# AdaLN block with an SSM layer and an eight-expert FFN: second modulated state kept as two fp32r parts, its shift folded into biases, b_out added by GpSimd, small VectorE operations moved to a PSUM bank

## The reference, cut to what matters

```python
# x (8, 1024, 128); c (8, 128); eight experts of 128x128
mod = (silu(c) @ wmod).reshape(8, 6, 1, 128)
sa, ca, ga, sb, cb, gb = (mod[:, i] for i in range(6))
ga, gb = guarded(ga), guarded(gb)            # sign * max(abs, 0.25)
h = layernorm(x) * (1 + ca) + sa
v, gate = split(h @ W_in + b_in)
s_t = sigmoid(A) * s_(t-1) + v_t             # scan over the 1024 steps of a batch
x = x + ga * ((sigmoid(gate) * s * C) @ W_out + b_out)
h = layernorm(x) * (1 + cb) + sb             # the second modulated state
p = softmax(h @ gate_w + gate_b)
w = where(p >= 0.1, p, 0); w = w / sum(w)
x = x + gb * sum_e w[e] * (h @ expert_w[e] + expert_b[e])
```

## Time and profile before

| | us |
|---|---|
| runs | 230.83, 226.45, 231.16 |
| median | 230.83 |
| the profiled execution's own time | 228.16 |
| its span in the trace | 226.4 |
| outside the span (228.16 - 226.4) | 1.76 |

### The profile page before, as it was taken

One profiled execution on the slowest core, in us unless ns is written; L12 is line 12 of the kernel. 1 busy time (PEld: TensorE's weight loads), 2 busy tenths in 40 slices (PEclk: granted clock), 3 DMA queues, 4 the chain that ended last, 5 costly groups with the idle time before them and its releaser, 6 DMA issues.

```text
span 226.4 us, 4220 instructions
## 1 busy us (share of the span) xinstructions
PE 204.2 (90%) x969; PEld 145.8 (64%) x969; DVE 211.0 (93%) x805; ACT 171.4 (76%) x546; POOL 149.5 (66%) x234
## 2 busy tenths in 40 slices
PE   0978869999999999999999999999999999989921
PEld 0863456868677777767686858585858685856700
DVE  5976799988999999999999999999999999998995
ACT  2332154989988889989898989898889799899910
POOL 8250055769586959697877869686868595766900
PEclk9999999999999999999999999999999999999985
DMA  6610011101103020201111111111010101001003
GB/s 210 150 35 0 0 47 49 42 8 51 46 2 91 4 88 6 63 30 51 46 48 48 49 48 46 46 49 48 1 46 3 46 0 48 4 1 46 19 28 93
DMA packets 19233, 9.82 MB, mean 43 GB/s; under 512 B 1305, under 2 KB 19082, under 8 KB 19210
## 3 DMA queue, kind: packets, MB, share of 16 engines
q1 hardware_dynamic: 17536, 9.03, 13.4%
q10 hardware_dynamic: 1674, 0.54, 0.9%
HBM read 5.37 MB, written 4.19 MB: 42 GB/s over the span
## 4 chain that ended last, share of the span: by engine, by line
PE 83%; DVE 7%; ACT 2%; issue 1%; DVEq 0%
PE ring L1520 14%; PE ring L1521 12%; PE ring L1522 12%; PE bank_g L1460 7%; PE bank_b L1503 7%; PE bank_v L1448 7%; PE bank_a L1479 6%; PE bank_b L1423 3%; PE bank_v L1449 3%; PE bank_a L1423 3%; DVE z L903 2%; PE bank_a L1481 2%; PE bank_b L1501 2%; PE bank_v L1544 1%; PE ring L1417 1%
## 5 line engine op out<-in xcount | busy, mean ns | idle before, releaser
L593 ACT ACTIVATE z<-ring,wts 128x128 f32<-128x128 f32 x436 | 121.8, 392 | 7.2 <-DVE wts L891 4.7
L443 POOL TENSOR_TENSOR z<-z 128x512 f32<-128x512 f32 x45 | 60.1, 1347 | 7.7 <-ACT z L593 7.7
L1520 PE MATMUL ring<-expert_w_hi,h_hi 128*128 128x512 f32 x128 | 62.0, 484 | 1.9 <-DVE z L903 0.7
L1522 PE MATMUL ring<-expert_w_hi,h_lo 128*128 128x512 f32 x128 | 50.5, 394 | 0.0
L1521 PE MATMUL ring<-expert_w_lo,h_hi 128*128 128x512 f32 x128 | 50.4, 394 | 0.0
L422 POOL TENSOR_SCALAR xn<-x,neg_mean,rstd 128x128 f32<-128x128 f32 x60 | 26.5, 455 | 33.2 <-DVE rstd L848 33.2
L411 POOL TENSOR_SCALAR xn<-x_in,neg_mean,rstd 128x128 f32<-128x128 f32 x56 | 25.0, 459 | 16.3 <-DVE rstd L848 16.3
L1520 PEld LDWEIGHTS ring<-expert_w_hi,h_hi 128*128 128x128 f32 x128 | 24.2, 189 | 14.4 <-issue 11.1
L964 DVE TENSOR_REDUCE mix<-z 128x256 f32<-128x1024 f32 x15 | 29.7, 1979 | 0.4 <-POOL z L443 0.4
L1521 PEld LDWEIGHTS ring<-expert_w_lo,h_hi 128*128 128x128 f32 x128 | 24.3, 190 | 5.5 <-issue 2.9
L1522 PEld LDWEIGHTS ring<-expert_w_hi,h_lo 128*128 128x128 f32 x128 | 24.1, 188 | 5.7
(11 more groups left out here) (122 smaller groups left out, 362.7 us busy)
## 6 DMA issues: line engine op xcount, KB each, us to landing
x_in<-in_L_attn_x_dram SPq DMA_DIRECT2D x16, 256.0 KB, 2.8
out_dram<-x SPq DMA_DIRECT2D x15, 256.0 KB, 2.3
expert_w<-in_L_ffn_expert_w_dram ACTq DMA_DIRECT2D x2, 256.0 KB, 3.3
wmod<-in_L_wmod_dram SPq DMA_DIRECT2D x1, 384.0 KB, 3.7
out_dram<-x SPq DMA_DIRECT2D x2, 128.0 KB, 1.9
expert_b<-in_L_ffn_expert_b_dram SPq DMA_DIRECT2D x12, 4.0 KB
w_in<-in_L_attn_W_in_dram SPq DMA_DIRECT2D x1, 128.0 KB, 3.9
w_out<-in_L_attn_W_out_dram SPq DMA_DIRECT2D x1, 64.0 KB, 3.6
```

The lines of the kernel that those rows point to most:

```text
L443: nc.gpsimd.tensor_tensor(z[:, g % 2, t, 0:4, :], z[:, g % 2, t, 0:4, :], z[:, g % 2, t, 4:8, :], ALU.add).then_inc(folded[t], 1)
L593: last = nc.scalar.activation(z[:, g % 2, t, e, :], bank_k[:, (e % 4) * P:(e % 4 + 1) * P], ACT.Copy, scale=wts[:, g % 2, t, e:e + 1])
L1520: mm(bank_k[:, :], hi, expert_w_hi[:, cols], start=True, stop=False)
L1522: mm(bank_k[:, :], lo, expert_w_hi[:, cols], start=False, stop=True).then_inc(e_ready[k], 1)
```

## The change

1. `h2_t` goes. `h2_high` scales the turned bank with 1+cb alone, without the shift sb; `low_part` computes bank*scale - high straight from PSUM. The shift goes into the biases per batch: sb @ gate_w and sb @ expert_w are computed once (`bias_rows`), added to the biases, split, and for the experts written to DRAM and read back in 12 small transfers into `expert_b_parts`. `logits` becomes twelve fp32r matmuls (three per tile), its bias matmul picks the batch's row.
2. ga*b_out leaves TensorE (L1481 goes). VectorE makes `gab_all` once; GpSimd adds it to `x_in` in place (`biased_input`, one 128x512 operation a group).
3. `second_norm` moves from GpSimd to ScalarE (four activations with `shift` = -mean*rstd as bias, a new small VectorE operation). `sum_fours` goes: GpSimd's `add_pairs` does both pairs and VectorE's `sum_pairs` both.
4. `bank_b` is given to VectorE as `scratch`; the turns of xn2 and the logits move to `bank_g`, the turned weights to `bank_v`. The root has one operation more.
5. The bias rows, `ones`, `pick` and `g_parts` grow from 33 or 40 rows to 96 (`ROWS`), filled with zeros.
6. SyncE issues the small loads that ScalarE issued; the three `picks` go; more `keep_clock` matmuls; new hand-written orders on all engines; in group 15 VectorE takes three halves, ScalarE five.

```diff
-LAST_DVE_HALVES = (1, 3, 5, 7)
+LAST_DVE_HALVES = (3, 5, 7)
+LAST_DVE_PAIRS = (1,)
+ROWS = 3 * PART
-        ones = sb("ones", [PART + 1, GROUP], F32R)
+        ones = sb("ones", [ROWS, GROUP], F32R)
-        bank_b = bank("bank_b")
+        scratch = bank("scratch")
+        mean_var = scratch_cols(0, 4 * TILES).rearrange("p (c k) -> p c k", k=2)
+        var_e = scratch_cols(4 * TILES, 2 * TILES)
...
+            def biased_input(g):
+                if g == 0:
+                    pool.wait_ge(gab_ready, RING)
+                pool.wait_ge(bn1_done, g + 1)
+                pool.wait_ge(xn1_ready, g + 1)
+                b = g // per_batch
+                nc.gpsimd.tensor_tensor(by_tile(x_in[:, g % SLOTS, :]), by_tile(x_in[:, g % SLOTS, :]),
+                                        gab_all[:, b:b + 1, :].to_broadcast([P, TILES, P]),
+                                        ALU.add).then_inc(biased_ready, 1)
...
-                nc.scalar.activation(h2_t[:, g % 2, :], bank_b[:, :], ACT.Identity,
-                                     bias=mod(2, g), scale=mod(3, g)).then_inc(h2_made, 1)
+                nc.scalar.activation(h2_hi[:, g % 2, :], bank_g[:, :], ACT.Copy, scale=mod(3, g)).then_inc(h2_ready, 1)
+            def second_norm(g):
+                act.wait_ge(shift_ready, g)
+                for j in range(TILES):
+                    last = nc.scalar.activation(
+                        tile(xn2, g % 2, j), tile(x1, g % SLOTS, j), ACT.Identity,
+                        bias=shift[:, g % 2, j:j + 1], scale=rstd[:, g % 2, j:j + 1])
+                last.then_inc(xn2_ready, 1)
...
-                vec.tensor_tensor(h2_lo[:, g % 2, :], h2_t[:, g % 2, :],
-                                  h2_hi[:, g % 2, :].bitcast(F32), ALU.subtract).then_inc(h2_split, 1)
+                vec.scalar_tensor_tensor(out=h2_lo[:, g % 2, :], in0=bank_g[:, :], scalar=mod_cols[:, 3, b:b + 1],
+                                         in1=h2_hi[:, g % 2, :].bitcast(F32), op0=ALU.mult,
+                                         op1=ALU.subtract).then_inc(h2_split, 1)
-                vec.tensor_reduce(mix[:, g % 2, pair, :],
-                                  z[:, g % 2, pair, 0:4, :].rearrange("p t e n -> p t n e"),
-                                  AX.X, ALU.add).then_inc(summed[i], 1)
...
-                mm(bank_a[:, :], pick_bf[:, b, :],
-                   gab_parts[:, :].unsqueeze(1).to_broadcast([3 * PART, TILES, P]),
-                   start=False, stop=True).then_inc(o_ready, 1)
+            def bias_rows():
+                mm(ring[0][0:batches, 0:experts], mod_cols[:, 2, :], gate_w[:, :], start=True, stop=True)
+                for h in range(2):
+                    last = mm(ring[2 + h][0:batches, :], mod_cols[:, 2, :], expert_w[:, h * 512:(h + 1) * 512],
+                              start=True, stop=True)
+                last.then_inc(bias_rows_done, 1)
...
+                mm(bank_x[:, 0:TE], pick[:, g // per_batch, :], gate_b_parts[:, :], start=True, stop=False)
                 for j in range(TILES):
+                    cols = bank_x[:, j * experts:(j + 1) * experts]
+                    mm(cols, tile(h2_hi, g % 2, j), gate_w_hi[:, :], start=False, stop=False)
+                    mm(cols, tile(h2_hi, g % 2, j), gate_w_lo[:, :], start=False, stop=False)
+                    last = mm(cols, tile(h2_lo, g % 2, j), gate_w_hi[:, :], start=False, stop=(j == TILES - 1))
...
+                sp.wait_ge(bias_low_ready, 1)
+                sp.dma_start(b_lo_d, expert_b_lo[:, :].bitcast(F32)).then_inc(bias_written, 16)
+                sp.wait_ge(bias_written, 16 * 2)
+                for part, rows in enumerate((b_hi_d, b_hi_d, b_lo_d)):
+                    for t in range(TILES):
+                        r = part * TE + t * experts
+                        sp.dma_start(expert_b_parts[r:r + experts, :, t * P:(t + 1) * P].bitcast(F32),
+                                     rows.rearrange("b (e n) -> e b n", e=experts)).then_inc(bias_in, 16)
```

1146 lines of the change are left out of this document (613 added, 533 removed), and 3 rows, old and new, of the table LAST_HALVES.

## The result

The changed kernel takes 225.83 us (median of 20 runs, 224.09 to 228.85) against 228.14 for the kernel before (20 runs, 226.30 to 232.30), 1.0% less. By the ratio the changed kernel takes 0.992 of the time of before, 95% interval 0.9892 to 0.9948. The forecast was 219.2 us and a gain of over 2%; the gain is 0.8%. The profiled execution took 226.16 us, of which its span in the trace is 224.3.

The account below looks back on a forecast made before the run. TensorE and VectorE were both full; afterwards TensorE would be longest. Start -3.5, steps -4.2, tail -2.6 make -10.3: span 226.4 to 216.1, 217.9 with 1.76 outside, 219.2 with half the 2.7 offset; range 212.5 to 227.0.

Parts of the forecast that it names:

- VectorE per step, 10.7: Loop: VectorE's work falls from 11.84 to 10.47 us, plus 0.2 for small operations in PSUM (bounds -0.2 to +0.9).
- TensorE per step, 11.1 to 11.15: Loop: TensorE's 11.43 us of work becomes 11.1, from -0.21, -0.39 and +0.28; 11.15 taken, the longest engine.
- Term (b): Loop, TensorE: the 96-row bias load of v is taken ahead, unlike the 33-row one, saving 0.39 us a step.
- The allowance of 0.2 for queueing: Loop: 0.2 us a step added to TensorE's 11.15 for waits on closer banks, giving a step of 11.35.
- a circle only over GpSimd and the norms: Loop: rstd, first norm, fold, pair sums, VectorE's operations, next root take 10.1 to 10.3 us, less than TensorE's 11.15.
- rival B: Loop: three banks for four and a VectorE-GpSimd circle turn TensorE's saving into waits; step 11.8, 222.1 to 223.3 us; chance 0.22.
- A: The forecast itself: a step of 11.35 us and a time of 219.2 us; chance 0.55.
- C: Loop: loads of short fp32r matmuls not hidden, 0.19 us each; step about 12.1, total 224.8 to 226; chance 0.13.
- D: Loop: GpSimd's queue ends the circle at the second pair sum; step 12.9, total 232 us; chance 0.10.
- The 11.55: Loop: step by the VectorE page's rule, near 11.55 us, placed between C and A.
- Start, -3.5: Start to group 4's product (64.56): 3.5 us earlier, first scan -3, group 0's low part -4.6; bounds -6 and +1.
- Tail, -2.6: Tail: TensorE -1.3 in groups 14 and 15, VectorE behind the last expert matmul -1.3; bounds -6 and 0.

Follow-up runs that it names:

- e1: Changed kernel with VectorE's small intermediate values in SBUF again instead of the PSUM bank; 254.14 us, 1.124 of the kernel before.
- e2: Changed kernel with the bias matmul of v reading 33 rows again instead of 96; 228.43 us, 0.999 of the kernel before.
- e13: Kernel before with only the bias matmul of v reading 96 rows instead of 33; 225.81 us, 0.993 of the kernel before.
- e4: Changed kernel with the shift of the second norm computed ahead of the scan; 226.03 us, 0.993 of the kernel before.
- e14: Kernel before with ten more empty matmuls ahead of TensorE's first turn; 227.68 us, 1.004 of the kernel before.
- e15: Kernel before with 96 rows in the bias matmul of v and ten more empty matmuls ahead of the first turn; 226.50 us, 0.996.
- e3: Changed kernel with the input of group 1 fetched ahead of the five vector loads on SyncE; 223.73 us, 0.982 of the kernel before.
- e17: Changed kernel with the gate's bias rows kept in the PSUM bank instead of SBUF; 223.90 us, 0.982 of the kernel before.
- e18: Changed kernel: group 1 input first, half before product, gate one half earlier, five empty matmuls, gate bias rows in PSUM, group 0 low part first; 221.03 us, 0.970.
- e16: Changed kernel with the start's experts' bias operations on VectorE and ScalarE cut to 8 columns; 225.71 us, 0.992 of the kernel before.
- e5: Changed kernel with group 15's second norm moved from ScalarE to VectorE and its shift left out; 230.51 us, 1.005 of the kernel before.
- e9: Changed kernel with group 15's second norm moved from ScalarE to GpSimd; 227.61 us, 0.990 of the kernel before.
- e10: Changed kernel with one VectorE reduction over four again for tiles 2 and 3 in groups 1 to 10; 242.15 us, 1.051 of before.

## Why the prediction was wrong, point by point

- **VectorE per step, 10.7:** 10.97 measured; 0.2 for the PSUM bank was near enough (the small groups differ by 13 ns or less from before), and the 0.9 worked out from the fixed cost of the Trainium skill ("VectorE: DVE Perf Modes", the TRN2 errata) isn't there. But the term asked the wrong question: it priced the bank and not what it avoids, which is 28 us in this order (e1). The clue stood in the earlier trace rows, GpSimd's idle 1.94 us at the very place of the small operations.
- **TensorE per step, 11.1 to 11.15:** its list is as forecast: 13 short matmuls 0.111 apart (1.34 to 1.45 us), no L1481, and the bias load under the matmul in front, though only 0.03 us ahead of its own and not 0.23. Term (b), -0.39, is the step of the forecast that failed in the loop: it was priced as if TensorE led the step. In the changed kernel, undoing it leaves the step at 11.58 (e2), in before, doing it leaves it at 11.82 (e13). The saving went into a wait for VectorE. In the start, where the forecast had no such term, the 96 rows do pay: 1.2 us of product 4 in the changed code (e2 against e4), 1.9 in the old (e14 against e15).
- **The allowance of 0.2 for queueing:** 0.47 measured. It should have been worked out as a circle: product, TensorE's list to the state input (9.3), scan and gating (2.17). I had drawn a circle only over GpSimd and the norms (10.1 to 10.3), which no run showed as the limit. Loop: -2.2 instead of -4.2. This is rival B's mechanism at about half of its price; B had 11.8, A 11.35, the step is 11.57. Rivals C and D didn't come (loads hidden, GpSimd's second pair sum in time, 9.8 us a step). The 11.55 that I had worked out from the Trainium skill's page "VectorE: DVE Perf Modes" was met by accident, through another mechanism.
- **Start, -3.5:** +0.4 in the profile. The first norm was to come 3 us earlier and came later, as the input of group 1 had moved behind five loads on SyncE: I had counted the loads taken off ScalarE's queue, not those that a moved load is queued behind (1.0 us, e3). The subtraction beside GpSimd cost 0.5 (e17). And the 64.56 that I subtracted from held 3.6 us of TensorE at half rate, to be seen in the earlier trace rows as 1.12 and 2.07 us for the same instruction; the 2.0 and 1.9 to 2.0 that I took off the path were durations at that rate. At equal clock product 4 is at 63.2 in the changed code (e4) and, by estimate, at 64.4 - 3.6 = 60.8 in the old, or at 63.2 - 1.8 = 61.4 (e14 less the fall of e15): there the change loses 1.8 to 2.4 us. The edits of e18 bring it to 61.9 with one half of 0.7 more ahead of it, 2.0 in all; they are the late input, the collision, and the statistics ahead of the low part. The experts' bias through DRAM cost nothing, inside my 0 to 2 (e16 and the idle time ahead of `mixed_bias(0)`).
- **Tail, -2.6:** -0.3 from product 13 on. VectorE's share behind the last expert matmul came (7.2 to 5.8 us, -1.4 for -1.3). TensorE's -1.3 didn't: from product 13 to the end of that matmul it takes 47.0 us in place of 45.9. The 2 x 0.65 was the loop's 0.47 a group and waits, so it carried the loop's mistake along; why the stretch grew by 1.1 us instead stays open: ScalarE is busy 40.64 of 42 us there, and taking 1.7 us off it didn't help (e5, e9), but both tests were spoilt by a collision and a fall of the clock.
- **The sum:** loop -2.2, start +0.4, tail -0.3 make the -2.1 of the spans (226.4 to 224.3), where -10.3 was forecast. Of the 8.2 us that are missing the start has 3.9, the tail 2.3 and the loop 2.0. At equal clock the changed profile loses another 1.7 (its fall at 34 to 39 us) and that of before 3.6, so by this estimate the change by itself is worth about 0.2 us; the measured 0.8% also holds how often each kernel's clock falls. The 1.3 us added for the offset of the profiled execution aren't there either: over 20 runs the median of before is 228.14, the profiled execution took 228.16.

## What to carry to other kernels

When engine sums lie close together, follow one buffer round the loop and add the latencies of each hand-over: a saving on an engine that waits inside such a circle was worth nothing here (0.39 us), and moving one piece of work into the wait was worth 0.17. Look at what GpSimd does while VectorE works on SBUF operands alone: a 160 ns operation lasted as long as the GpSimd instruction beside it (1.27 us), and one operand in PSUM cured it. Before subtracting from a measured milestone, compare the same instruction's duration in two stretches, or a slow clock is counted as work.

## What the runs showed of the hardware

- A VectorE operation with its operands in SBUF was held up by a GpSimd addition beside it: 8 columns 1.27 us for 0.17 (L872 in e1), `sum_pairs` 1.51 for 0.42 (e10), four 128x128 norms 3.05 for 1.17 (e5). The scratch in SBUF cost 34 us of VectorE's busy time (229.5 against 195.2). With one operand in PSUM none was held up (L1019 687 ns in e1), and neither was a `TENSOR_REDUCE` with one SBUF input (0.17 to 0.19 us beside the folds of e1); beside GpSimd's norm little was lost (0.14 to 0.21).
- TensorE ran at half rate from 13.8 to 20.5 us in before (2.07 us for a matmul that takes 1.12) while the granted clock was shown as 1.00; in other profiles the fall is shown (0.50 at 36 to 38 us). With the first gap filled by empty matmuls the half rate there was gone, and a fall at 28 to 39 us stood in its place (0.91 and 0.77 in e14 over 28 to 34 and 34 to 39 us).
- The 96-row weight load of the bias matmul starts 0.03 us before its matmul, under the matmul in front; from the start of the state input to the next piece it is 1.08 us. With 33 rows the load starts with the matmul, and it is 1.37 (e2).
